# Each piece of the adaptive gates goes to all 128 partitions by one transfer in place of four

## The reference

```python
# block 0: adaptive layer norm with gates
tp = (silu(cond) @ Wt + bt)[:, None, :]
shift_msa, scale_msa, gate_msa, shift_mlp, scale_mlp, gate_mlp = split(tp, 6, axis=-1)
h = layernorm(x, g1, be1) * (1.0 + scale_msa) + shift_msa
x = x + gate_msa * attention(h)            # 16 heads of 8 features, output projection Wproj
h = layernorm(x, g2, be2) * (1.0 + scale_mlp) + shift_mlp
x = x + gate_mlp * (gelu(h @ W1 + b1) @ W2 + b2)
# block 1: RMS norm, scale and shift from cond (film), no gates
h = film(rmsnorm(x, norm1_w), cond, film1_w, film1_b)
x = x + attention_1_head(h)                # q, k, v, proj
h = film(rmsnorm(x, norm2_w), cond, film2_w, film2_b)
x = x + gelu(h @ mlp_w1 + mlp_b1) @ mlp_w2 + mlp_b2
```

## Time and profile before

| | us |
|---|---|
| median of 3 runs | 260.62 |
| lowest and highest | 259.19, 263.34 |
| the profiled execution | 260.67 |
| its span in the profile | 258.8 |

### The profile page before, as it was taken

One profiled execution on the slowest core, in us unless ns is written; L12 is line 12 of the kernel. 1 busy time (PEld: TensorE's weight loads), 2 busy tenths in 40 slices (PEclk: granted clock), 3 DMA queues, 4 the chain that ended last, 5 costly groups with the idle time before them and its releaser, 6 DMA issues.

```text
span 258.8 us, 10297 instructions
## 1 busy us (share of the span) xinstructions
PE 237.8 (92%) x3952; PEld 179.4 (69%) x3952; DVE 165.6 (64%) x509; ACT 148.7 (57%) x338; POOL 151.0 (58%) x161
## 2 busy tenths in 40 slices
PE   0588888997999998999999999999999999999995
PEld 0556566876778775687766669877776666777775
DVE  4868997888899999374454455478887444542002
ACT  2368566666767658925566545646566665444440
POOL 7442543855857768776666776797675545553110
PEclk9999999999999999999999999999999999999999
DMA  6963333423443443440000000000000011101112
GB/s 211 317 235 96 98 97 96 143 62 128 108 131 107 128 121 82 114 144 20 3 0 0 0 0 0 1 5 3 0 0 3 0 42 43 40 0 43 41 41 84
DMA packets 17451, 18.01 MB, mean 70 GB/s; under 512 B 2320, under 2 KB 13072, under 8 KB 17296
## 3 DMA queue, kind: packets, MB, share of 16 engines
q1 hardware_dynamic: 16848, 15.67, 20.9%
q10 hardware_dynamic: 576, 1.98, 2.2%
HBM read 11.48 MB, written 4.59 MB: 62 GB/s over the span
## 4 chain that ended last, share of the span: by engine, by line
PE 75%; DVE 7%; DMA 5%; SPq 5%; issue 3%; ACT 3%; POOL 1%; ACTq 0%; POOLq 0%; DVEq 0%
PE bank L1135 22%; PE bank L951 19%; PE bank L927 5%; PE bank L995 4%; PE bank L1025 3%; PE bank L1142 3%; PE bank L1145 3%; DMA values_scratch<-Vs 3%; PE bank L1175 3%; PE bank L1046 2%; PE bank L1007 2%; SPq L257 2%; DMA X<-x 2%; SPq L268 2%; ACT xhat L762 2%
## 5 line engine op out<-in xcount | busy, mean ns | idle before, releaser
L762 ACT ACTIVATE xhat<-X,shift,rstd 128x128 f32 (+1 forms) x96 | 40.3, 485 | 50.7 <-POOL shift L327 50.7
L1135 PE MATMUL bank<-W,Kx 128*128 128x128 f32 x512 | 59.6, 275 | 0.0
L1135 PEld LDWEIGHTS bank<-W,Kx 128*128 128x128 f32 x512 | 58.5, 192 | 1.0 <-issue 1.0
L951 PE MATMUL bank<-h,W 128*128 128x512 f32 x124 | 56.5, 595 | 0.1
L338 POOL TENSOR_TENSOR h<-hA,B 128x512 f32<-128x512 f32 x32 | 33.5, 1047 | 30.9 <-DVE hA L498 30.7
L817 ACT ACTIVATE Kx<-bank,col 128x512 f32<-128x512 f32 x64 | 39.2, 676 | 8.9 <-PE bank L951 8.9
L498 DVE TENSOR_TENSOR hA<-bank,A 128x512 f32<-128x512 f32 x32 | 21.7, 679 | 30.4 <-PE bank L927 15.0
L951 PEld LDWEIGHTS bank<-h,W 128*128 128x128 f32 x124 | 22.2, 190 | 21.8 <-issue 21.5
L346 POOL TENSOR_TENSOR Ss<-Sc,smax 128x512 f32<-128x512 f32 x16 | 16.8, 1050 | 26.3 <-DVE smax L524 26.1
L325 POOL TENSOR_TENSOR rstd<-v_sb,minus_half 128x4 f32<-128x4 f32 x24 | 24.6, 1024 | 11.7 <-DVE v_sb L483 6.6
L927 PEld LDWEIGHTS bank<-ident,xhat 128*128 128x128 f32 x128 | 15.9, 147 | 13.2 <-issue 8.8
(11 more groups left out here) (124 smaller groups left out, 392.7 us busy)
## 6 DMA issues: line engine op xcount, KB each, us to landing
values_scratch<-Vs SPq DMA_DIRECT2D x8, 288.0 KB, 2.3
Vx<-values_scratch SPq DMA_DIRECT2D x32, 72.0 KB, 2.0
gate<-gates_scratch SPq DMA_DIRECT2D x32, 64.0 KB, 2.2
gate<-gates_scratch SPq DMA_DIRECT2D x16, 128.0 KB, 2.6
out<-X SPq DMA_DIRECT2D x7, 256.0 KB, 2.3
Kx<-Ks SPq DMA_DIRECT2D x24, 64.0 KB, 1.9
W<-weights ACTq DMA_DIRECT2D x1, 1152.5 KB, 6.0
X<-x SPq DMA_DIRECT2D x4, 256.0 KB, 7.0
```

Of the source, the lines that this page charges most:

```text
L762: last = act.activation(xhat[:, p, P * t:P * (t + 1)], X[:, x_tile(gg, t), :], ACT.Identity, bias=shift[:, p, t:t + 1], scale=rstd[:, p, t ...
L951: last = pe.matmul(bank[2 + n][:, :], w(f"W1_{phase // 2}", n), h[:, p, :], start=True, stop=True)
L1135: last = pe.matmul(y[t // 2][:, P * t:P * (t + 1)], gT[:, p, n, P * t:P * (t + 1)], w(f"W2_{phase // 2}", n), start=(n == 0), stop=(n == N ...
```

## The change

Each piece is moved by one transfer. Its destination is all 128 partitions of the piece; its source is the piece of `gates_d` with the four sequences outermost and a broadcast dimension of 32 behind them. The semaphore `gates_in[i]` thus grows by 16 for each piece in place of 64, and the waits on it are changed to match.

```diff
--- before.py
+++ after.py
@@ -272,11 +272,10 @@
 
                 size = NT // pieces
                 tiles = slice(n * size, (n + 1) * size)
-                wait(sp, gates_in[i], 16 * TB * n)
-                for b in range(TB):
-                    sp.dma_start(gate[L * b:L * (b + 1), i, tiles, :].rearrange("p t d -> p (t d)"),
-                                 gates_d[b:b + 1, i, tiles, :].rearrange("o t d -> o (t d)")
-                                 .broadcast_to([L, size * D])).then_inc(gates_in[i], 16)
+                wait(sp, gates_in[i], 16 * n)
+                sp.dma_start(gate[:, i, tiles, :].rearrange("p t d -> p (t d)"),
+                             gates_d[:, i, tiles, :].rearrange("b t d -> b (t d)").unsqueeze(1)
+                             .broadcast_to([TB, L, size * D])).then_inc(gates_in[i], 16)
 
             sp.wait_ge(gate_ready, 1)
             for b in range(TB):
@@ -383,7 +382,7 @@
                 if known(g, 0, NG - 1):
                     subtract_max(g + 1, 0)
                 if not first:
-                    pool.wait_ge(gates_in[0], 16 * TB * g)
+                    pool.wait_ge(gates_in[0], 16 * g)
                     add_gated(0, g - 1)
 
             def scale_rows(gg, p):
@@ -417,7 +416,7 @@
                     if phase == 1 and first:
                         power(gg + 3, 1 - p)
                         add_shift(gg + 2, p, phase, g)
-                        pool.wait_ge(gates_in[0], 16 * TB * NG)
+                        pool.wait_ge(gates_in[0], 16 * NG)
                         add_gated(0, 7)
                         return
                     if phase == 1 or known(g, 0, 6):
@@ -428,7 +427,7 @@
                         power(gg + 3, 1 - p, NG)
                     if phase == 1:
                         if p == 1:
-                            pool.wait_ge(gates_in[1], 8 * TB * (g + 1))
+                            pool.wait_ge(gates_in[1], 8 * (g + 1))
                         add_gated(1, g - 1)
                     else:
                         keep(phase, g, p)
```

## The result

| | before | after |
|---|---|---|
| median, us | 260.85 (22 runs) | 262.28 (22 runs) |
| lowest and highest, us | 259.19, 263.34 | 260.86, 266.81 |
| the profiled execution, us | 260.67 | 263.60 |
| its span, us | 258.8 | 261.7 |

The ratio is 1.0063, 95% interval 1.004 to 1.0087: the change makes the kernel slower by 0.4 to 0.9%. The ratio is taken over the fast runs alone (266.09 and 266.81 us are slow ones), so it is not the quotient of the two medians. The forecast was 260.4 us, 0.2 us less than before; the time moved the other way. The 262.28 us lie inside the range of 258.8 to 263.4 us, whose top had been set for rival 1. The profiled execution of the changed kernel was 1.3 us slower than its median, so its +2.9 us of span overstate the loss by about a factor of two; the profile is used for where the time goes, the ratio for how much.

The account below looks back on a forecast made before the run. PE work was taken to bound 75% of the span; 0.1 us from group 3's earlier store plus 0.1 us of the 1.4 us wait made 0.2 us off 260.62: 260.4 us, range 258.8 to 263.4.

Parts of the forecast that it names:

- rival 1: Gate transfers confined to four engines, the store of the values queued behind them: 261.2 us, or 265 us; chance 0.38.
- The step that failed: Gate transfers on SP's queue: bytes unchanged by merging, four times 64 KB or once 256 KB.
- the collision of group 3: Group 3's store of the values landing late, 4.38 us; bounded at 1.4 us won and 2.2 us lost.
- SP's cycle: Under rival 1, SP's step per group takes 9.95 us, where PE needs 9.85 and 9.6 us.
- the low rate: Under rival 1, 23.9 GB/s for each busy engine, 2.7 us of data per piece, giving 261.2 us.
- 0.9 of 1.2 us covered: Under rival 1, group 4's store lands at 65.6 for 64.4, 0.9 us covered; price 0.4 us at group 5.
- SP's issue time: Issuing a merged gate piece on SP: 0.45 us, bounds 0.34 and 1.98; some 1.5 us less per group.
- 2.0 of the 2.1 us are turned into a wait: At group 3, SP then waits for ACT's values, so the store starts only 0.1 us sooner.
- The late landing of group 3: Group 3's store took 4.38 us to land; the four pieces ahead are not the cause; 1.4 us at most to win.
- Rival 2: Late landing of group 3's store goes, and PE's 1.4 us wait with it: 259.2 us; chance 0.10.
- The gates' readers: POOL reads gate 1's piece 0 at 109.19 us; it lands in time, on four engines at 107.9 us.
- The waits of PE: Sign that the forecast is wrong and rival 1 holds: PE waits for Kx or Vx in groups 5 to 7.

Follow-up runs that it names:

- e1: The changed kernel with each gate row standing four times in DRAM, so a 16-row source on sixteen engines; ratio 0.9987 to the kernel before.
- e4: The kernel before with gate 0 sent by two transfers of 64 partitions per piece, each on two engines; ratio 1.0622.
- e9: The kernel before without gate 0 transfers; POOL multiplies by a constant row, awaited after its first steps; output differs; ratio 0.9991.
- e2: The kernel before with only the pieces of gate 1 merged into one transfer each, gate 0 as before; ratio 0.9983.
- e6: The kernel before, four transfers per piece, with gate 0 pieces issued behind the next store of the values instead of ahead; ratio 0.9920.
- e11: The kernel before without the second load of weights and ACT's wait for it, so part of the MLP uses other weights; ratio 0.9997.
- e12: The kernel e6 without the second load of weights and ACT's wait for it; ratio 0.9945 to the kernel before.
- e5: The changed kernel with each gate 0 piece issued behind the next store of the values instead of ahead; ratio 0.9982 to the kernel before.
- e8: The kernel before without gate 0 transfers; POOL waits for a constant row at its very beginning, so the start is late; ratio 1.0018.

## Why the prediction was wrong, point by point

- **The step that failed** is the one that left the engines out of the sum: "The bytes are the same: four times 64 KB or once 256 KB", with the landing of the store bounded only by the collision of group 3, as one chance late landing. The count of 1600 shows four engines for each piece, the stores of the values land in 4.7 us in place of 2.3 (median), PE waits 4.1 us for Kx and Vx in place of 1.4, and e1 (same merge, sixteen engines) brings the time back to 0.9987. That 262.28 us lies inside the range is due to rival 1, for which the range had been widened. The prediction had the mechanism as rival 1, with a chance of 0.38, and the evidence for it was the shape of the source in the diff, since the trace of before holds no such transfer. By the rule of the Trainium skill quoted there ("DMA: Bandwidth & Descriptors", section "Why a DMA increments its semaphore by 16 and not by 1") the number is the largest up to 16 that divides both slowest dimensions: 4 for the change, 16 for e1, 2 for e4. All three counts agree with it (1600, 1808, 1840). A rule that gives the very number deserved more than the rows that could not speak of it.
- **Rival 1, its terms.** Rate for each engine: 23.9 GB/s worked out, 24 measured. Landing of the store after the piece's issue: 5.5 worked out, 5.8 measured (70.96 to 76.79). SP's cycle: 9.95 us worked out, 10.1 and 10.9 measured (66.68, 76.81, 87.72). Its time: 261.2 at the low rate, 262.3 measured. What was too small is the sum over groups: 0.4 us once and 0.1 to 0.3 three times, while in the profile PE waits for the keys five times, 3.4 us in all, already from group 3 on. At group 5 the prediction calls 0.9 of 1.2 us covered, though by its own rows the keys land at 70.8 us at the latest and PE needs them at 71.05, so that only some 0.3 us were; PE waited 0.8 us there. And the 261.2 takes the low end of its own terms: 260.6 + 0.4 + 0.3 to 0.9 - 0.2 is 261.1 to 261.7 us. On sixteen engines, too, a piece takes longer than its 0.7 to 0.9 us of data and 2.0 us would make it: 4.0 us in e1.
- **SP's issue time.** Taken at 0.45 us for a merged piece, bounds 0.34 and 1.98; measured 0.58. "2.0 of the 2.1 us are turned into a wait" held: SP's wait for ACT's values at line 263 is 2.8 us before, 5.3 in the changed kernel and 10.5 in e1.
- **The late landing of group 3** was said not to come from the pieces ahead of it. e9 confirms it, with 4.6 us and no pieces. Rival 2 (it goes) did not happen in the changed kernel: 5.4 us there (51.03 to 56.43). But it does go in some executions of other kernels, for some 1.2 us, near the 1.4 that the prediction gave it.
- **The gates' readers.** Piece 0 of gate 1 was to be ahead of POOL even on four engines, 7.5 us from issue to landing; it took 8.5 (103.83 to 112.29) and was ahead by less than 0.1 us, so this came right by little; e2 shows that gate 1 costs nothing.
- **The waits of PE** were named as what would show the forecast wrong ("waits of PE for Kx or Vx in groups 5 to 7"), and they did.

## What to carry to other kernels

Fewer transfers are not fewer microseconds: look first whether the issuing queue is waited for at all, and here an engine's values were what it waited for. Before two or more transfers are merged, look at the outermost count of the source: here 16, 4 and 2 put the data on as many engines, and the small packets of the profile tell it (16, 4 or 2 completions for each transfer). A narrow transfer is harmless where nothing that matters stands behind it; so when a queue mixes a deadline and bulk, try to issue the deadline first and to put the bulk into the wait for its landing, which here won 0.8% (e6; why it is so much isn't shown) where the merge lost 0.6%.

## What the runs showed that I had not expected

- Sixteen engines do not bring a merged piece in at once: a piece of 256 KB lands 4.0 us after its issue in e1 (median), while each of four pieces of 64 KB lands in 2.2 us, the last issued 1.5 us after the first. Merging gains nothing in landing even at full width.
- The cost of narrowness is not linear: 16, 4 and 2 engines give landings of the store of 2.3, 4.7 and 7.2 us, but ratios of 1, 1.006 and 1.062; with two engines the granted clock falls as well.
- The order of SP alone is worth more than the number of its transfers: e6 moves the issues of seven pieces and changes none, and is the fastest kernel of the study, although leaving those transfers out altogether (e9) gives 0.9991. That e6 is faster than e9 I can't explain. Some 1.2 us would come of it if the store of group 3 landed late in most executions of one and seldom in the other, but with one profiled execution for each kernel the record doesn't show how often it does.
- One landing costs 1.2 us or not by the execution: the store of group 3 takes 4.3 to 4.9 us in the profiles of before, e1, e2, e9, e11 and e12, and 2.2 to 2.6 in those of e5 to e8.
